# Attention scores of a graph network layer: destination rows from a reversed scan of on-chip rows instead of gathers, batches in descending order

## The chip, the core and the metric

The kernel runs on one core of a Trainium2 chip. The metric is device time in microseconds (us). A core has five engines, each with its own instruction queue: PE (TensorE, matmuls and transposes), DVE (VectorE), ACT (ScalarE), POOL (GpSimd, here the issuer of the indirect DMAs that gather or scatter rows) and SP (SyncE, here the issuer of plain DMAs). They meet through semaphores alone. SBUF is the on-chip memory, PSUM the eight banks that PE writes.

## What is computed

Four graph layers over 50,000 nodes of 128 numbers and 25,000 edges that are sorted by destination; after each layer the result is added to x and normalised row by row. The change concerns the third layer:

```python
h = jnp.einsum('nd,rde->rne', x, W)              # W: 8 relations, 128 x 128
h_src, h_dst = h[edge_type, src], h[edge_type, dst]
attn = jnp.sum(h_src * h_dst, axis=-1)
attn = jax.nn.leaky_relu(attn, negative_slope=0.2)
# softmax of attn over the edges of each type -> a
out = jax.ops.segment_sum(h_src * a[:, None], dst, num_segments=N)
```

## The kernel before

The edges are padded to 49 batches (`NB`) of 512 (`BE`), each of four tiles (`BT`) of 128. The stages run one after the other, with a barrier between them: setup (columns of flags and row numbers), prefill, CONV1, CONV2, MEAN, attention scores, softmax, ATTEND, SUM. In MEAN, ATTEND and SUM (`edge_stage`) a batch's gathered source rows are turned on PE into columns, DVE writes a copy for each relation in which only that relation's edges are not zero (`masked`, L1302), PE multiplies it by that relation's weights and adds up (L1225), DVE sums over equal destinations with a forward scan (L1323), and PE turns the sums back into rows (L1215).

MEAN leaves two things for the attention stage. The table X2 in HBM holds one finished row for each node; for a node with edges it is the row written at its last edge. The SBUF buffer `m.xd` holds, for each of the 25,088 edge places, the row that MEAN computed at that place; only at the last edge of a destination is that the destination's finished row.

The attention stage (`attention_stage`) computes x_dst (W_r W_rᵀ) x_src for each edge. After `ww` = W_r W_rᵀ is made, each of the 49 batches passes through:

- ACT writes the row numbers as integers, of the sources and of the destinations (L1518, L1519, `gi`).
- POOL gathers 4 tiles of source rows and 4 tiles of destination rows, one indirect DMA each (L1496, `rows`). SP stores the source rows to `source_rows` for ATTEND (L1479).
- PE transposes all 8 tiles (L1575) into the banks `T[0]` and `T[1]`; ACT copies both to SBUF (L1529, L1530, `col`). There is one such pair of banks, so the next batch's transposes wait for these copies.
- DVE makes 8 masks from the destination columns (L1592), PE multiplies each by `ww` (L1553, 16 instructions a batch, since each f32 matmul is two), DVE multiplies the sum by the source columns (L1603, `prod`), and PE adds that over the 128 features against a column of ones (L1564); ACT keeps the four columns of scores (L1523).

The order on each engine is the order of the code in its `body(b, q)`, which serves several batches at once: PE's body b does the scores of batch b-2, relations 0 to 3 of batch b, the transposes of b+1, relations 4 to 7 of b. `rows`, `gi` and `typ` have two slots, so the gathers for batch s wait until batch s-2 has been turned and its source rows stored. `hold` is a wait on SP or POOL.

## Time and profile before

| what | value |
|---|---|
| median of 3 runs | 3763.21 us (3763.13 to 3765.24) |
| profiled execution, its own time | 3760.51 us |
| its span, first to last instruction | 3758.6 us |
| PE busy | 2909.0 us, 77% |
| DVE busy | 2965.8 us, 79% |
| POOL busy | 1858.1 us, 49% |
| attention stage, first gather to last score | 1986.8 to 2521.3 us |

The profiled execution is one run of its own; its time stands 2.7 us under the median of the other three. Busy shares are means over stages that have different limits, so they don't say what bounds the attention stage.

### The profile page before, as it was taken

What the parts mean: (1) busy time and instruction counts of PE and PEld (TensorE: products, weight loads), DVE (VectorE), ACT (ScalarE), POOL (GpSimd) and SP (SyncE); (2) the same over time, 40 slices, a digit from 0 to 9 for tenths busy, and PEclk for the clock granted to TensorE, in tenths of its full rate; (3) what the DMA queues carried; (4) which work ended last, traced back from release to release, by engine and by line L of the source; (5) the groups of instructions that cost most, each with busy time, mean ns of one, the idle gap of its engine ahead of it and who ended that gap; (6) DMA issues with size and microseconds to landing.
All of it is one profiled execution on the core that took longest, in us unless ns stands there. A gap on an engine that the chain in (4) does not pass through costs nothing. (4 is left out here: it accounts for less than half of the span.)

```text
span 3758.6 us, 57586 instructions
## 1 busy us (share of the span) xinstructions
PE 2909.0 (77%) x10747; PEld 1631.2 (43%) x10747; DVE 2965.8 (79%) x8628; ACT 1678.5 (45%) x4665; POOL 1858.1 (49%) x1779
## 2 busy tenths in 40 slices
PE   2665664666655566799986888877999899999997
PEld 1433443555545555344433444443343344444443
DVE  7886555999969999699983555557999878888886
ACT  2775775888857677455541111113444411111111
POOL 2775776444434443355536777750000046666664
PEclk9998887889878887799998999988999999999998
DMA  2664444555545655233322222222222211111111
GB/s 64 198 194 147 150 150 134 190 198 199 198 139 193 197 185 186 94 92 92 92 82 80 87 88 86 83 61 66 92 92 85 86 49 45 46 50 49 50 53 34
DMA packets 267148, 418.71 MB, mean 111 GB/s; under 512 B 54780, under 2 KB 116537, under 8 KB 267082
## 3 DMA queue, kind: packets, MB, share of 16 engines
q1 hardware_dynamic: 210634, 318.80, 25.9%
q0 software_dynamic: 56448, 99.21, 9.5%
q8 instruction: 20, 0.33, 0.0%
q14 instruction: 46, 0.38, 0.0%
HBM read 215.60 MB, written 206.07 MB: 112 GB/s over the span
## 5 line engine op out<-in xcount | busy, mean ns | idle before, releaser
L1225 PE MATMUL bank<-sum_masked,sum_w 128*128 128x512 f32 x1568 | 691.1, 594 | 1.4 <-DVE sum_masked L1302 1.4
L1112 POOL DMA_INDIRECT sum_rows<-t_x,sum_gi x196 | 228.1, 1164 | 691.8 <-ACT sum_gi L1136 646.7
L1302 DVE SCALAR_TENSOR_TENSOR sum_masked<-sum_typ,sum_col 128x512 f32<-128x512 bf16 x784 | 487.9, 683 | 18.9 <-ACT sum_col L1155 16.9
L1496 POOL DMA_INDIRECT at_rows<-t_x,at_gi x392 | 391.5, 999 | 172.9 <-issue 124.5
L1592 DVE SCALAR_TENSOR_TENSOR at_masked<-at_typ,at_col 128x512 f32<-128x512 bf16 x392 | 247.0, 691 | 260.1 <-ACT at_col L1530 234.6
L1225 PEld LDWEIGHTS bank<-sum_masked,sum_w 128*128 128x128 f32 x1568 | 291.2, 191 | 332.2 <-issue 271.3
L1225 PE MATMUL bank<-mean_masked,mean_w 128*128 128x512 f32 x784 | 377.5, 612 | 18.8 <-DVE mean_masked L1302 18.8
L1225 PE MATMUL bank<-att_masked,att_w 128*128 128x512 f32 x784 | 380.4, 613 | 9.7 <-DVE att_masked L1302 7.7
L1553 PE MATMUL bank<-at_masked,at_ww 128*128 128x512 f32 x784 | 377.7, 627 | 1.9 <-DVE at_masked L1592 1.9
L1112 POOL DMA_INDIRECT mean_rows<-t_x,mean_gi x196 | 224.0, 1143 | 232.8 <-ACT mean_gi L1136 185.4
L1112 POOL DMA_INDIRECT c_rows<-t_g,c_gi x196 | 187.1, 955 | 274.9 <-ACT c_gi L1136 138.3
L920 ACT ACTIVATE c_dense_x<-c_dense_z,c_dense_shift,c_dense_scale 128x128 f32<-128x128 f32 x784 | 311.5, 480 | 16.9 <-DVE c_dense_shift L965 16.6
L1112 POOL DMA_INDIRECT c_rows<-x_dram,c_gi x196 | 189.6, 967 | 225.4 <-ACT c_gi L1136 177.5
L1155 ACT ACTIVATE sum_col<-bank 128x512 f32<-128x512 f32 x49 | 29.3, 597 | 571.4 <-PE bank L1265 571.4
L1120 POOL DMA_INDIRECT out_dram<-sum_new,sum_si x196 | 239.2, 1220 | 84.1 <-issue 57.9
L1302 DVE SCALAR_TENSOR_TENSOR mean_masked<-mean_typ,mean_col 128x512 f32<-128x512 bf16 x392 | 250.1, 680 | 17.7 <-ACT mean_col L1155 17.6
L1302 DVE SCALAR_TENSOR_TENSOR att_masked<-att_typ,att_col 128x512 f32<-128x512 bf16 x392 | 250.4, 681 | 12.7 <-ACT att_col L1155 12.4
L628 POOL DMA_INDIRECT pf_ds<-t_info,pf_gi x196 | 194.5, 992 | 84.6 <-issue 61.4
L626 POOL DMA_INDIRECT pf_xs<-x_dram,pf_gi x196 | 200.6, 1023 | 63.5 <-issue 57.4
L1553 PEld LDWEIGHTS bank<-at_masked,at_ww 128*128 128x128 f32 x784 | 150.6, 202 | 157.3 <-issue 126.7
L1225 PEld LDWEIGHTS bank<-mean_masked,mean_w 128*128 128x128 f32 x784 | 130.2, 190 | 197.1 <-DVE mean_masked L1302 153.0
L1225 PEld LDWEIGHTS bank<-att_masked,att_w 128*128 128x128 f32 x784 | 130.1, 190 | 191.1 <-DVE att_masked L1302 147.0
(289 smaller groups left out, 5696.2 us busy)
## 6 DMA issues: line engine op xcount, KB each, us to landing
t_x<-c_dense_x SPq DMA_DIRECT2D x196, 256.0 KB, 3.7
pf_xc<-x_dram SPq DMA_DIRECT2D x98, 256.0 KB, 3.0
t_g<-pf_g SPq DMA_DIRECT2D x98, 256.0 KB, 3.1
t_x<-pf_x SPq DMA_DIRECT2D x98, 256.0 KB
c_dense_x<-t_x SPq DMA_DIRECT2D x98, 256.0 KB, 3.8
out_dram<-c_dense_x SPq DMA_DIRECT2D x98, 256.0 KB, 4.0
c_same<-p_same SPq DMA_DIRECT2D x98, 128.0 KB, 3.5
t_g<-c_new SPq DMA_DIRECT2D x49, 256.0 KB
```

Of the source, the lines that this page charges most:

```text
L626: pool.indirect_dma_start(xs[:, q, j, :], None, io["x"], index).then_inc(gathered[q], 16)
L628: pool.indirect_dma_start(ds[:, q, j, :], None, m.info_table, index).then_inc(gathered[q], 16)
L920: last = act.activation(rows[:, q, j, :], self.z[:, q, j, :], ACT.Identity, bias=self.shift[:, q, i, j:j + 1], scale=self.scale[:, q, i, j ...
L1112: pool.indirect_dma_start(rows[:, q, j, :], None, source, bass.IndirectOffsetOnAxis(ap=gi[:, q, j:j + 1], axis=0))\
L1120: pool.indirect_dma_start(out, bass.IndirectOffsetOnAxis(ap=si[:, qs, j:j + 1], axis=0), new[:, qs, j, :], None, bounds_check=NP - 1, oob_ ...
L1155: act.activation(col[:, o, :], T[o][:, :], ACT.Copy).then_inc(col_ready, 1)
L1225: pe.matmul(H[q][:, :], w[:, r, :], masked[:, r % MASKS, :], start=(r == 0), stop=(r == n_rel - 1))\
L1302: v.scalar_tensor_tensor(out=masked[:, r % MASKS, :], in0=typ[:, q, :], scalar=float(r), in1=col[:, q, :], op0=ALU.is_equal, op1=ALU.mult) ...
L1496: pool.indirect_dma_start(rows[:, q, side, j, :], None, m.tables["X2"], bass.IndirectOffsetOnAxis(ap=gi[:, q, side, j:j + 1], axis=0))\
L1553: pe.matmul(U[q][:, :], ww[:, r, :], masked[:, r % MASKS, :], start=(r == 0), stop=(r == R8 - 1))\
L1592: v.scalar_tensor_tensor(out=masked[:, r % MASKS, :], in0=typ[:, q, :], scalar=float(r), in1=col[:, q, 1, :], op0=ALU.is_equal, op1=ALU.mu ...
```

## The change

The attention stage gathers only the source rows. The destination rows come from `m.xd`: ACT copies the batch's four tiles multiplied by a column that is 1 at the last edge of a destination and 0 elsewhere (`ends_col`, L1506 after the change), so all other rows become zero; PE transposes them into banks of their own (`turn_dst`, L1551), and DVE spreads each finished row back over all edges of its destination with a scan that runs from the last column to the first (`last_rows_back`, L1604), steered by a plane that is 1 where the next edge has the same destination (`next_plane`, loaded by SP). The scan carries its value from batch to batch, so the batches run from 48 down to 0. The roles of the two sides swap: the masks are made of the source columns, and `prod` multiplies by the destination columns. Setup loses the computation of the last edge's row number and its column, and gains the plane and the column of flags.

```diff
-        SRC_F, CL_F, LAST_F, DINV_F, T8_F, DST_F, WEIGHT_F, END_F = range(8)
+        SRC_F, CL_F, LAST_F, DINV_F, T8_F, DST_F, WEIGHT_F = range(7)
...
-            for f, plane in enumerate((m.same_plane, m.type_plane[R8], m.type_plane[R16])):
+            for f, plane in enumerate((m.same_plane, m.type_plane[R8], m.type_plane[R16], m.next_plane)):
                 sp.dma_start(plane.rearrange("(q n) -> q n", n=256), typ[:, f, :]).then_inc(stored, 16)
-            hold(sp, stored, 48)
+            hold(sp, stored, 64)
...
+            v.tensor_copy(typ[:, 3, :], nxt[:, :])
...
-            v.wait_ge(numbered, 1)
-            link(v.scalar_tensor_tensor(out=end[:, :], in0=cnt[:, 1, R8, :], scalar=-1.0, in1=number[:, :],
-                                        op0=ALU.add, op1=ALU.add))
-            link(slot_rows(v, end_rows, end[:, :]))
-            link(v.tensor_tensor(own[:, :], end_rows[:, 0, :], end_rows[:, 1, :], ALU.add))
-            v.scalar_tensor_tensor(out=field[:, END_F, :], in0=own[:, :], scalar=float(NP), in1=end_rows[:, 2, :],
-                                   op0=ALU.add, op1=ALU.add)
...
-            v.wait_ge(colC, 8)
+            v.wait_ge(colC, 7)
+            v.tensor_scalar(m.ends_col[:, :], m.last_col[:, :], float(FAR), None, ALU.is_lt)
...
+        T, TD, U, SC, WB = m.psum[0:2], m.psum[2:4], m.psum[4:6], m.psum[6:8], m.psum[2:4]
         LAST = NB - 1
+        batch = lambda s: s * -1 + LAST
...
                 if runs(s, 0, LAST):
                     if runs(s, 2):
                         hold(sp, mask_ready, (s - 1) * R8)
-                    plane = m.type_plane[R8][bass.ds(s * BE, BE)]
-                    sp.dma_start(typ[:, q, :], plane.rearrange("(a n) -> a n", a=1).to_broadcast([P, BE]))\
-                        .then_inc(typ_loaded[q], 16)
+                        hold(sp, dst_ready, s - 1)
+                    sp.dma_start(typ[:, q, :], spread(m.type_plane[R8], s)).then_inc(typ_loaded[q], 16)
+                    sp.dma_start(nxt[:, q, :], spread(m.next_plane, s)).then_inc(nxt_loaded[q], 16)
                 s = b + 1
                 if runs(s, 0, LAST):
-                    hold(sp, gathered[1 - q], of_slot(s, 1 - q, 32 * BT))
-                    sp.dma_start(m.source_rows[:, bass.ds(s * BE, BE)],
-                                 rows[:, 1 - q, 0].rearrange("p b d -> p (b d)")).then_inc(stored[1 - q], 16)
+                    hold(sp, gathered[1 - q], of_slot(s, 1 - q, 16 * BT))
+                    sp.dma_start(m.source_rows[:, bass.ds(batch(s) * BE, BE)],
+                                 rows[:, 1 - q].rearrange("p b d -> p (b d)")).then_inc(stored[1 - q], 16)
...
-                        hold(pool, turned, s - 1)
+                        hold(pool, src_turned, s - 1)
                         hold(pool, stored[q], of_slot(s - 2, q, 16))
-                    for side in range(2):
-                        for j in range(BT):
-                            pool.indirect_dma_start(rows[:, q, side, j, :], None, m.tables["X2"],
-                                                    bass.IndirectOffsetOnAxis(ap=gi[:, q, side, j:j + 1], axis=0))\
-                                .then_inc(gathered[q], 16)
+                    for j in range(BT):
+                        pool.indirect_dma_start(rows[:, q, j, :], None, m.tables["X2"],
+                                                bass.IndirectOffsetOnAxis(ap=gi[:, q, j:j + 1], axis=0))\
+                            .then_inc(gathered[q], 16)
...
                     if runs(s, 2):
-                        act.wait_ge(gathered[q], of_slot(s - 2, q, 32 * BT))
-                    act.activation(gi[:, q, 0, :], at(m.row_col, s), ACT.Copy)
-                    act.activation(gi[:, q, 1, :], at(m.end_col, s), ACT.Copy).then_inc(idx_ready, 1)
+                        act.wait_ge(gathered[q], of_slot(s - 2, q, 16 * BT))
+                    act.activation(gi[:, q, :], at(m.row_col, batch(s)), ACT.Copy).then_inc(idx_ready, 1)
+                    if runs(s, 2):
+                        act.wait_ge(dst_turned, s - 1)
+                    for j in range(BT):
+                        last = act.activation(ends[:, q, j, :], m.xd[:, bass.ds(batch(s) * BE + j * D, D)], ACT.Copy,
+                                              scale=m.ends_col[:, bass.ds(batch(s) * BT + j, 1)])
+                    last.then_inc(ends_ready, 1)
...
-                    act.wait_ge(turned, s + 1)
+                    act.wait_ge(src_turned, s + 1)
                     if runs(s, 2):
-                        act.wait_ge(prod_ready, s - 1)
-                    act.activation(col[:, o, 0, :], T[0][:, :], ACT.Copy)
-                    act.activation(col[:, o, 1, :], T[1][:, :], ACT.Copy).then_inc(col_ready, 1)
+                        act.wait_ge(mask_ready, (s - 1) * R8)
+                    act.activation(col[:, o, :], T[o][:, :], ACT.Copy).then_inc(col_ready, 1)
...
+            def turn_dst(s, q):
+                if not runs(s, 0, LAST):
+                    return
+                pe.wait_ge(ends_ready, s + 1)
+                if runs(s, 2):
+                    pe.wait_ge(dst_ready, s - 1)
+                for j in range(BT):
+                    last = pe.transpose(TD[q][:, j * TE:(j + 1) * TE], ends[:, q, j, :], m.ident[:, :])
+                last.then_inc(dst_turned, 1)
+
...
-                    pe.wait_ge(gathered[o], of_slot(s, o, 32 * BT))
-                    if runs(s, 1):
-                        pe.wait_ge(col_ready, s)
-                    for side in range(2):
-                        for j in range(BT):
-                            last = pe.transpose(T[side][:, j * TE:(j + 1) * TE], rows[:, o, side, j, :], m.ident[:, :])
-                    last.then_inc(turned, 1)
+                    pe.wait_ge(gathered[o], of_slot(s, o, 16 * BT))
+                    if runs(s, 2):
+                        pe.wait_ge(col_ready, s - 1)
+                    for j in range(BT):
+                        last = pe.transpose(T[o][:, j * TE:(j + 1) * TE], rows[:, o, j, :], m.ident[:, :])
+                    last.then_inc(src_turned, 1)
+                turn_dst(s, o)
                 relate(b, q, range(R8 // 2, R8))
...
-                                           in1=col[:, q, 1, :], op0=ALU.is_equal, op1=ALU.mult).then_inc(mask_ready, 1)
+                                           in1=col[:, q, :], op0=ALU.is_equal, op1=ALU.mult).then_inc(mask_ready, 1)
+
+            def last_rows_back(s, q):
+
+                if not runs(s, 0, LAST):
+                    return
+                v.wait_ge(nxt_loaded[q], of_slot(s, q, 16))
+                v.wait_ge(dst_turned, s + 1)
+                if runs(s, 1):
+                    v.wait_ge(dst_ready, s)
+                if runs(s, 2):
+                    v.wait_ge(prod_ready, s - 1)
+                start = 0.0 if static(s) and s == 0 else dst[:, 1 - q, 0:1]
+                v.tensor_tensor_scan(dst[:, q, ::-1], nxt[:, q, ::-1], TD[q][:, ::-1], start, ALU.mult, ALU.add)\
+                    .then_inc(dst_ready, 1)
...
                 s = b - 1
                 if runs(s, 0, LAST):
                     v.wait_ge(mask_used, (s + 1) * R8)
+                    v.wait_ge(dst_ready, s + 1)
                     if runs(s, 2):
                         v.wait_ge(scored, s - 1)
-                    v.tensor_tensor(prod[:, o, :], col[:, o, 0, :], U[o][:, :], ALU.mult).then_inc(prod_ready, 1)
+                    v.tensor_tensor(prod[:, o, :], dst[:, o, :], U[o][:, :], ALU.mult).then_inc(prod_ready, 1)
+                last_rows_back(b, q)
                 relate(b, q, range(R8 // 2, R8))
```

On PE, two bodies that stand written out ahead of the loop. The names are those of the tiles: `at_masked` the masks, `at_prod` the products, `at_rows` the gathered rows, `at_ends` the flagged rows of `m.xd`. Before:

```order
L1553 MATMUL bank<-at_masked,at_ww 128x512 x4
L1564 MATMUL bank<-m_ones,at_prod 128x1 x4
L1553 MATMUL bank<-at_masked,at_ww 128x512 x4
L1575 MATMUL bank<-m_ident,at_rows 128x128 x8
L1553 MATMUL bank<-at_masked,at_ww 128x512 x4
L1564 MATMUL bank<-m_ones,at_prod 128x1 x4
L1553 MATMUL bank<-at_masked,at_ww 128x512 x4
L1575 MATMUL bank<-m_ident,at_rows 128x128 x8
L1553 MATMUL bank<-at_masked,at_ww 128x512 x4
```

and after:

```order
L1541 MATMUL bank<-at_masked,at_ww 128x512 x4
L1562 MATMUL bank<-m_ones,at_prod 128x1 x4
L1541 MATMUL bank<-at_masked,at_ww 128x512 x4
L1572 MATMUL bank<-m_ident,at_rows 128x128 x4
L1551 MATMUL bank<-m_ident,at_ends 128x128 x4
L1541 MATMUL bank<-at_masked,at_ww 128x512 x4
L1562 MATMUL bank<-m_ones,at_prod 128x1 x4
L1541 MATMUL bank<-at_masked,at_ww 128x512 x4
L1572 MATMUL bank<-m_ident,at_rows 128x128 x4
L1551 MATMUL bank<-m_ident,at_ends 128x128 x4
L1541 MATMUL bank<-at_masked,at_ww 128x512 x4
```

The eight transposes of gathered rows have become four of gathered rows and four of `at_ends`, behind a wait of their own; nothing else on PE has moved.

On SP, the issues of the batches written out ahead of the loop, before:

```order
L1479 DMA source_rows<-at_rows 128x512
L1474 DMA at_typ<-p_type 128x512
L1479 DMA source_rows<-at_rows 128x512
L1474 DMA at_typ<-p_type 128x512
L1479 DMA source_rows<-at_rows 128x512
L1474 DMA at_typ<-p_type 128x512
```

and after (`at_nxt` is the plane's slot):

```order
L1464 DMA source_rows<-at_rows 128x512
L1459 DMA at_typ<-p_type 128x512
L1460 DMA at_nxt<-p_next 128x512
L1464 DMA source_rows<-at_rows 128x512
L1459 DMA at_typ<-p_type 128x512
L1460 DMA at_nxt<-p_next 128x512
L1464 DMA source_rows<-at_rows 128x512
```

One more load stands in front of each store of the source rows.

On DVE, the first batches, written out ahead of the loop (x8 is masks 4 to 7 of one batch and 0 to 3 of the next), before:

```order
L1592 SCALAR_TENSOR_TENSOR at_masked<-at_typ,at_col 128x512 x12
L1603 TENSOR_TENSOR at_prod<-at_col,bank 128x512
L1592 SCALAR_TENSOR_TENSOR at_masked<-at_typ,at_col 128x512 x8
L1603 TENSOR_TENSOR at_prod<-at_col,bank 128x512
L1592 SCALAR_TENSOR_TENSOR at_masked<-at_typ,at_col 128x512 x8
```

and after:

```order
L1590 SCALAR_TENSOR_TENSOR at_masked<-at_typ,at_col 128x512 x4
L1604 SCALAR_TENSOR_TENSOR at_dst<-at_nxt,bank 128x512
L1590 SCALAR_TENSOR_TENSOR at_masked<-at_typ,at_col 128x512 x8
L1616 TENSOR_TENSOR at_prod<-at_dst,bank 128x512
L1604 SCALAR_TENSOR_TENSOR at_dst<-at_nxt,at_dst,bank 128x512
L1590 SCALAR_TENSOR_TENSOR at_masked<-at_typ,at_col 128x512 x8
L1616 TENSOR_TENSOR at_prod<-at_dst,bank 128x512
```

Behind each product the scan (the order prints a scan as SCALAR_TENSOR_TENSOR; `at_dst` is its output) has come in, ahead of masks 4 to 7.

## Rows read from the trace of the kernel before

**Rows 1.** Busy time in stretches: attention stage, then MEAN (PEclk is the granted clock)

```profile
1987.00:2520.00 533.00, 458.94 (x1560) 244.59 (x1560) 273.92 (x441) 70.02 (x239) 391.24 (x392) 0.93 0.28 84
1563.00:1965.00 402.00, 381.90 (x1114) 165.38 (x1114) 377.20 (x938) 204.40 (x552) 204.15 (x176) 1.00 0.30 89
```

**Rows 2.** Waits between 2010 and 2510 us: us in total, times, longest

```profile
PE bank L1575 <- DMA at_rows<-t_x,at_gi: 59.0, 33, 3.1
```

**Rows 3.** The gathers by tile: duration ns min/median/max, first and last start

```profile
L1496 POOL DMA_INDIRECT at_rows<-t_x,at_gi x392: 938/944/1459, 1986.8 to 2503.8; - x196
```

**Rows 4.** Timeline of a batch that waited: start us, us, engine, line

```profile
2347.45 1.97 PE L1575 MATMUL bank<-m_ident,at_rows 128*128 128x128 f32 x8 [2.92 <-DMA at_rows<-t_x,at_gi]
2349.21 5.70 PE L1553 MATMUL bank<-at_masked,at_ww 128*128 128x512 f32 x8
```

**Rows 5.** Stretch of the same batch, columns as in Rows 1

```profile
2348.00:2350.00 2.00, 2.00 (x8) 1.55 (x7) 0.00 (x0) 0.55 (x2) 1.39 (x3) 0.50 0.50 174
```

**Rows 6.** Timeline of PE in a batch that never waited

```profile
2355.55 3.68 PE L1553 MATMUL bank<-at_masked,at_ww 128*128 128x512 f32 x8
2359.07 1.04 PE L1575 MATMUL bank<-m_ident,at_rows 128*128 128x128 f32 x8
2359.94 3.60 PE L1553 MATMUL bank<-at_masked,at_ww 128*128 128x512 f32 x8
2363.38 0.95 PE L1564 MATMUL bank<-m_ones,at_prod 128*128 128x1 f32 x8
2364.19 3.68 PE L1553 MATMUL bank<-at_masked,at_ww 128*128 128x512 f32 x8
```

**Rows 7.** Timeline of ACT: score copy of batch 0 and of batch 46

```profile
2023.68 0.17 ACT L1523 ACTIVATE m_score_col<-bank 128x4 f32<-128x4 f32 x1 [2.95 <-PE bank L1564]
2512.35 0.17 ACT L1523 ACTIVATE m_score_col<-bank 128x4 f32<-128x4 f32 x1 [3.14 <-PE bank L1564]
```

**Rows 8.** DVE beside the PE of Rows 6, and ACT's column copy

```profile
2364.04 0.68 DVE L1603 TENSOR_TENSOR at_prod<-at_col,bank 128x512 f32<-128x512 f32 x1
2364.64 2.49 DVE L1592 SCALAR_TENSOR_TENSOR at_masked<-at_typ,at_col 128x512 f32<-128x512 bf16 x4
2368.78 0.60 ACT L1529 ACTIVATE at_col<-bank 128x512 f32<-128x512 f32 x1 [4.14 <-PE bank L1575]
```

**Rows 9.** Scans: setup forward, setup backward, MEAN forward from PSUM

```profile
22.09 0.67 DVE L392 TENSOR_TENSOR_SCAN su_cnt<-su_flag,su_relid 98x256 f32<-98x256 f32 x1
22.67 0.67 DVE L393 TENSOR_TENSOR_SCAN su_cnt<-su_flag,su_relid 98x256 f32<-98x256 f32 x1
L1323 DVE TENSOR_TENSOR_SCAN mean_run<-mean_same,mean_run,bank x48: 1278/1279/1281, 1557.6 to 1960.8; 128x512 f32<-128x512 bf16 x48
```

**Rows 10.** Timeline: ACT's scaled row copies in ATTEND, four tiles

```profile
2704.37 1.28 ACT L1148 ACTIVATE att_scaled<-att_rows,m_alpha_col 128x128 f32<-128x128 f32 x4 [3.10 <-DMA att_rows<-source_rows]
```

**Rows 11.** Timeline of the SUM stage: one group of four transposes, then relations

```profile
3410.55 0.60 PE L1215 MATMUL bank<-m_ident,sum_run 128*128 128x128 f32 x4
3410.98 7.03 PE L1225 MATMUL bank<-sum_masked,sum_w 128*128 128x512 f32 x16
```

**Rows 12.** DMA issues, 1990 to 2510 us: KB each, median us to landing

```profile
source_rows<-at_rows SPq DMA_DIRECT2D x49, 256.0 KB, 2.6
```

**Rows 13.** Timeline of the stage's start

```profile
1990.51 0.94 POOL L1496 DMA_INDIRECT at_rows<-t_x,at_gi  x1 [0.30 <-issue]
1995.50 0.94 POOL L1496 DMA_INDIRECT at_rows<-t_x,at_gi  x1 [0.30 <-issue]
1998.11 1.94 PE L1575 MATMUL bank<-m_ident,at_rows 128*128 128x128 f32 x8 [12.92 <-DMA at_rows<-t_x,at_gi]
2001.95 5.33 PE L1553 MATMUL bank<-at_masked,at_ww 128*128 128x512 f32 x8 [1.90 <-DVE at_masked L1592]
```

**Rows 14.** Timeline of setup on DVE: destination row numbers, up to the next sum

```profile
41.90 0.42 DVE L415 SCALAR_TENSOR_TENSOR su_end<-su_cnt,su_number 98x256 int32<-98x256 f32 x1
43.89 2.55 DVE L421 TENSOR_TENSOR su_cnt<-su_cnt 98x2304 f32<-98x2304 f32 x1
```

More of the change, by code:

```diff
@@ L322, in setup_stage @@
         carry = sb("carry", [QR, 2, R8 + 1])
-        field = sb("field", [QR, 8, 256])
-        typ = sb("typ", [QR, 3, 256], BF16)
+        field = sb("field", [QR, 7, 256])
+        typ = sb("typ", [QR, 4, 256], BF16)
         own = sb("own", [QR, 256])
@@ L327, in setup_stage @@
         rooted = sem("rooted")
-        numbered = sem("numbered")
-        number = sb("number", [QR, 256])
-        end = sb("end", [QR, 256], I32)
-        end_rows = sb("end_rows", [QR, 3, 256], I32)
         ps = m.psum
@@ L466, in _ @@
             pe.wait_ge(lin, 2)
-            for f in range(8):
+            for f in range(7):
                 for b in range(2):
@@ L1444, in attention_stage @@
         MASKS = 8
-        gi = sb("gi", [P, 2, 2, BT], I32)
-        rows = sb("rows", [P, 2, 2, BT, D])
-        typ = sb("typ", [P, 2, BE], BF16)
-        col = sb("col", [P, 2, 2, BE])
+        gi = sb("gi", [P, 2, BT], I32)
+        rows = sb("rows", [P, 2, BT, D])
+        typ, nxt = sb("typ", [P, 2, BE], BF16), sb("nxt", [P, 2, BE], BF16)
+        col, dst = sb("col", [P, 2, BE]), sb("dst", [P, 2, BE])
+        ends = sb("ends", [P, 2, BT, D])
         masked = sb("masked", [P, MASKS, BE])
@@ L1466, in _, with spread @@
             sp.dma_start(w[:, :, :], io["W_att"].rearrange("r i o -> i r o")).then_inc(w_loaded, 16)
+            def spread(plane, s):
+                return plane[bass.ds(batch(s) * BE, BE)].rearrange("(a n) -> a n", a=1).to_broadcast([P, BE])
             def body(b, q):
@@ L1711, in build @@
         m.dstraw_col, m.hi_col, m.lo_col, m.ds_col, m.score_col = map(column, ("dstraw", "hi", "lo", "ds", "score"))
-        m.weight_col, m.alpha_col, m.row_col, m.end_col = map(column, ("weight", "alpha", "row", "end"))
+        m.weight_col, m.alpha_col, m.row_col, m.ends_col = map(column, ("weight", "alpha", "row", "ends"))
         m.node = sb("node", [P, RPP])
```

19 lines of the change are left out of this document (8 added, 11 removed).

## The prediction

> **What bounds the kernel now.** I read the page's slices first: the attention stage lies between MEAN and softmax, and in it no engine is busy throughout. The windows say how far off PE is: 459 of 533 us busy at a mean granted clock of 0.93, where MEAN, with the same eight relations a batch, has 382 of 402 us at 1.00 [rows 1]. So PE is idle or slowed for part of the stage, and the question is what it waits for. The chain of what ended last is of no help here, as it lies in SUM and says nothing of an earlier stage; the waits inside the stage are. PE waits 59.0 us for the gathers, in 33 waits, the longest 3.1 us [rows 2].
>
> Then the gathers themselves: 392 of them start between 1986.8 and 2503.8 us, one each 517.0 / 391 = 1.322 us, though one lasts 0.944 [rows 3]. Eight a batch make 8 x 1.322 = 10.58 us. The score copies give the stage's rhythm: from that of batch 0 at 2023.68 to that of batch 46 at 2512.35 are 46 intervals, 10.62 us each [rows 7]. The two agree within 0.4%: **POOL's issue of the gathers is the bound**, with no room in it.
>
> PE pays twice for it. A batch that waited 2.92 us for its gathers turned its rows in 1.97 us and ran 8 matmul instructions in 5.70 [rows 4], with the granted clock at 0.50, that is 1.2 GHz [rows 5]; a batch without the wait took 1.04 and 3.60 for the same [rows 6]. Such a batch then runs late, and the next ones catch up. What PE needs when it never waits is in Rows 6: from one batch's first relation at 2355.55 to the next's at 2364.19 are **8.64 us** (3.52 for four relations, 0.87 for eight transposes, 3.44 for four relations, 0.81 for the scores). That is the floor of PE at 2.4 GHz.
>
> **What the change does to each engine, per batch.** POOL: four gathers of eight go, so 4 x 1.322 = 5.3 us of issue remain where 10.6 were. That is well under 8.64, so POOL no longer bounds, unless its waits do (below).
>
> PE: four transposes of gathered rows become four of flagged rows, the rest is the same; what is new is a second group with a wait of its own. SUM shows what a group of four costs when PE is the bound: from 3410.55 to 3410.98, 0.43 us [rows 11], so two groups are 0.86 against 0.87 for one of eight. I take 8.64. The other bound is that such a group costs the whole 0.60 us of its row instead of 0.43, if its wait keeps it from overlapping what follows: 0.17 us more, 8.81.
>
> DVE: adds the scan. Eight masks take 2 x 2.49, the product 0.68 [rows 8]. The scan isn't in the trace as it will run, backward from a PSUM bank. Two rows are near: MEAN's forward scan from PSUM of the same 512 elements takes 1.279 us, and setup's 256-element scans take 0.67 us forward and 0.67 backward [rows 9]. Direction costs nothing there, so I take 1.28; the upper end, twice the rate lost, is 2.56. Sum 4.98 + 0.68 + 1.28 = 6.9 us, below 8.64. Its place matters more than its sum: it stands between the product and masks 4 to 7. Counted from the start of PE's scores at 2363.38, the product starts at +0.66 and ends its turn at +1.26 [rows 6, 8]; the scan holds DVE to +2.54, mask 4 is there at about +3.2, masks 4 to 7 end at +5.0. PE asks for mask 4 at 0.81 + 3.52 + 0.87 = +5.2. There are 2.0 us to spare; a scan of 2.56 us leaves 0.7, so both ends give the same time. Masks 0 to 3 of the next batch need ACT's column copy, which comes at about +5.4 once four transposes, not eight, are done; they end by +8.0, before PE asks at +9.4.
>
> ACT: one column copy (0.60 [rows 8]) goes, four scaled row copies come, 1.28 us for the four in ATTEND [rows 10]. Together with the small ones some 2.3 us of work in 8.64. They are made a batch ahead, and wait only for transposes that PE has passed. They cost nothing, hidden by PE's matmuls; without that cover 1.3 us.
>
> SP: one more plane load per batch, ahead of the store of the source rows, and a wait for the scan. Behind that store the gathers two batches on wait, so this is the queue to check. Masks of batch b are done at +5.0 of body b, later than the scan, so the new wait is never the last. Allow 1 us for the two loads' issue (my choice, more than any issue here seems to need): the store goes out at +6.2 and lands 2.6 us later [rows 12], at +8.8. The gathers of batch b+3 then start, four at 1.322, the last at +12.8, and its rows come 2.6 us after its start (1995.50 to 1998.11 [rows 13]), at +15.4. PE wants them in body b+2, at 2 x 8.64 + 4.33 = +21.6. There are 6 us to spare.
>
> So no wait is left on PE, and with none the clock should stay where MEAN has it. **The stage's 46 intervals: 46 x (10.62 - 8.64) = 91.1 us less.**
>
> At this point the Trainium skill (TensorE: Matmul & The Clock Gate, section "HAM oscillation — how this bites in real kernels") tells of a matmul loop whose waits on DMAs each let the clock gate throttle PE, so that the next tile starts cold. The trace agrees: 2.92 us of wait, then 0.50. By that page the second payment of each wait goes too, which is within the 91.1.
>
> **The stage's start.** The first transposes wait for the last of batch 0's gathers. It was the eighth, started at 1995.50; now it is the fourth, as at 1990.51 [rows 13], 4.99 us earlier. Transposes at the low clock took 1.94 for eight, and two column copies stood before the first mask; with four (0.97) and one copy of 0.60 [rows 8], of which I count 0.5 as the two overlap a little, the first relation comes 1.47 us earlier again, at 2001.95 - 6.46 = 1995.49. From there to the score copy of batch 0 were 21.73 us, with waits for the next batches' gathers. Without them: 5.33 for the first eight instructions at the low clock [rows 13], 0.87 + 3.52 to the end of the batch, 8.64 - 0.81 for batch 1, and 0.95 for the scores ahead of the copy: 18.5. So 3.2 us less, 9.7 us for the start.
>
> **Setup.** The row numbers of the last edges go: 43.89 - 41.90 = 1.99 us [rows 14], and one copy of a column. Added are a copy to the plane and the column of flags. No row shows these three; at the 0.42 us of L415 each they come to 0.42 more added than removed, so 1.6 us less in sum, and 2.4 with the two new ones at nothing. I take 1.9, all on DVE's chain that ends setup.
>
> **Sum.** 91.1 + 9.7 + 1.9 = 102.7, from 3760.5, the profiled execution's own time: 3657.8. The median of the runs lies 2.7 us higher, which makes 3660.5; with some tenths for stray waits (a choice) I say 3661. All other stages have the same instructions.
>
> **Rivals.**
> 1. *PE still waits at times (SP's store or a group's wait late).* For it: before, each wait of 2 to 3 us cost as much again in clock, so the price per case is high. Against: 6 us to spare on the gathers and 2 on the masks. With the 8.81 bound at each batch it is 46 x 0.17 = 8 us: 3669. If every fourth batch lost 4 us (a wait and its low clock), 46: about 3707. Chance 0.10.
> 2. *The clock stays low without waits.* The skill's same page (section "A second HAM failure mode: psum-queue depth-cycling") has short idles between groups of matmuls, cycling through PSUM banks, make the clock oscillate. As a mechanism here: PE goes through four pairs of banks per batch, and breaks off before each group. Were the granted clock 0.93 as now, an interval would be 8.64 / 0.93 = 9.29, and 46 x 0.65 = 30 us are lost: 3691. Against it: MEAN cycles through its banks at 1.00 [rows 1]. Chance 0.05.
> 3. *The backward scan from PSUM is slow.* Up to some 3.3 us (1.28 + 2.0 to spare) it costs nothing. Beyond, DVE delays masks 4 to 7 by each us, and over a batch sum of 8.64 it is the bound. To end **slower than before**, the interval must exceed 10.62 + 11.5 / 46 + 0.16 = 11.0 us, so the scan 11.0 - 5.7 = 5.3 us, four times MEAN's. Setup's equal pair speaks against it; that pair read SBUF, not PSUM, so it doesn't exclude it. A scan of 4.5 us would give about 46 x 1.5 = 69 us over forecast, 3730. Chance 0.02 for slower, 0.01 for between.
> 4. *No change*: PE's wait is put on the gathers, but something else of 10.6 us is behind. Only POOL has a sum near it. Chance 0.02.
>
> **How the numbers follow.** Forecast 0.80, rivals 0.10, 0.05, 0.03 (0.01 and 0.02) and 0.02. The forecast's own range is 3654 (the start and setup at their best, no stray wait) to 3669 (8.81 each). To leave out no more than 2 in 10, the range goes up into rival 1 but not to rival 2's end: 3652 to 3686. A measurement of this kernel tells 0.2% or 7.5 us from no change. Faster: the forecast, rivals 1 and 2 and the 0.01 of rival 3, 0.96; same 0.02; slower 0.02.
>
> **What would show it.** Right: score copies 8.6 to 8.8 us apart, the granted clock 1.00 in the stage, no wait of PE on `at_rows`, POOL idle for about 3 us a batch, a scan near 1.28 us, DVE waiting for ACT's column copy as before but briefly, and the stage's last score near 2419 us. Wrong: a wait of PE on masks 4 or `at_ends` (the scan or ACT is late), on `at_rows` (SP's store), or long relations without a wait (the clock).

## The result, and the profile after

The changed kernel takes 3679.86 us (median of 4 runs, 3675.34 to 3687.97) against 3763.17 (4 runs, 3761.50 to 3765.24) before: ratio 0.9781, 95% interval 0.9762 to 0.9799. That is faster, inside the forecast's range (3652 to 3686) but 19 us above its 3661. The profiled execution took 3677.66, with a span of 3675.9, so it is 82.8 us shorter than that of before, where the sum had said 102.7. The question is where 20 us are.

Windows of the trace after: attention stage, its steady part, MEAN. Columns as in [rows 1].

```profile
1985.00:2520.00 535.00, 487.52 (x1734) 262.14 (x1735) 408.18 (x635) 128.26 (x406) 196.37 (x195) 0.95 0.28 81
2010.00:2400.00 390.00, 390.00 (x1446) 215.16 (x1444) 306.22 (x452) 91.95 (x310) 181.34 (x180) 1.00 0.31 92
1558.00:1960.00 402.00, 383.74 (x1122) 166.26 (x1120) 377.67 (x938) 204.68 (x552) 204.66 (x176) 1.00 0.31 89
```

The first row spans what the stage took before, and runs on into ATTEND. The second is the one to read: PE is busy for 390.00 of 390.00 us at a granted clock of 1.00, the upper of its two levels, 2.4 GHz. POOL is busy for 181 of 390 us (46%), where it was for 391 of 533 (73%) in [rows 1].

Four of the waits after, 2010 to 2400 us (total, times, longest):

```profile
ACT at_col L1518 <- PE bank L1572: 169.7, 45, 3.8
POOL at_rows L1480 <- DMA source_rows<-at_rows: 164.5, 45, 4.5
DVE at_masked L1590 <- ACT at_col L1518: 57.3, 45, 1.4
DVE at_prod L1616 <- PE bank L1541: 25.9, 45, 0.7
```

The view has no wait of PE itself in this stretch, neither on `at_rows`, as in [rows 2], nor on anything else. All four waiters here are engines with time over. POOL now waits for the store of the source rows, 164.5 / 45 = 3.7 us a batch, for which nobody waits in turn.

The tiles, after: gathers, the backward scan, the score copies (duration in ns min/median/max, first and last start).

```profile
L1480 POOL DMA_INDIRECT at_rows<-t_x,at_gi x196: 938/944/1468, 1983.5 to 2396.9; - x196
L1604 DVE TENSOR_TENSOR_SCAN at_dst<-at_nxt,at_dst,bank x48: 1272/1274/1275, 2004.4 to 2409.3; 128x512 f32<-128x512 bf16 x48
L1512 ACT ACTIVATE m_score_col<-bank x49: 173/173/174, 2012.3 to 2418.3; 128x4 f32 x42, 128x4 f32<-128x4 f32 x7
```

The scan backward from PSUM takes 1274 ns, MEAN's forward one 1279 [rows 9]. One batch in the timeline (start, duration, engine, line), which answers to [rows 6] and [rows 8]:

```profile
2201.28 0.95 PE L1562 MATMUL bank<-m_ones,at_prod 128*128 128x1 f32 x8
2201.57 0.69 DVE L1616 TENSOR_TENSOR at_prod<-at_dst,bank 128x512 f32<-128x512 f32 x1 [0.57 <-PE bank L1541]
2202.09 3.68 PE L1541 MATMUL bank<-at_masked,at_ww 128*128 128x512 f32 x8
2202.18 1.27 DVE L1604 TENSOR_TENSOR_SCAN at_dst<-at_nxt,at_dst,bank 128x512 f32<-128x512 bf16 x1
2202.49 0.94 POOL L1480 DMA_INDIRECT at_rows<-t_x,at_gi  x1 [3.26 <-DMA source_rows<-at_rows]
2203.37 2.51 DVE L1590 SCALAR_TENSOR_TENSOR at_masked<-at_typ,at_col 128x512 f32<-128x512 bf16 x4
2205.61 0.60 PE L1572 MATMUL bank<-m_ident,at_rows 128*128 128x128 f32 x4
2206.05 0.60 PE L1551 MATMUL bank<-m_ident,at_ends 128*128 128x128 f32 x4
2206.49 3.60 PE L1541 MATMUL bank<-at_masked,at_ww 128*128 128x512 f32 x8
```

The order on DVE is product, scan, masks 4 to 7, as reckoned. The two groups of transposes stand 0.44 us apart (0.43 was taken). The score copies follow each other in 8.63 or 8.64 us, and the last is at 2418.33, where the prediction had "near 2419"; before it was at 2521.16. **So the whole gain was there at the end of the attention stage: 102.8 us.** Twenty microseconds of it are lost behind it, in code that the change doesn't touch.

`att_sd` is computed once a batch in ATTEND. Its row shows how long the stage takes; the second row is ACT's idle time until the source rows have landed, the third is PE's idle time until ACT's scaled copies of them are there (us, times). First before, then after:

```profile
L1175 ACT ACTIVATE att_sd<-att_mv,m_eps x49: 281/288/297, 2584.7 to 2996.3; 128x4 f32<-128x4 f32 x49
  DMA att_rows<-source_rows: 157.3, 48
  PE bank L1265: 19.0, 16
```

```profile
L1161 ACT ACTIVATE att_sd<-att_mv,m_eps x49: 282/288/298, 2482.1 to 2912.8; 128x4 f32<-128x4 f32 x49
  DMA att_rows<-source_rows: 177.4, 48
  PE bank L1251: 36.2, 32
```

411.6 us have become 430.7, 8.97 a batch where it was 8.58, at a granted clock of 1.00 in both. PE waits 17.2 us more for the scaled copies. One load of the source rows and the scaled copies that wait for it, after; before, the copies started 3.57 us after the load's issue (2700.80 to 2704.37, [rows 10]):

```profile
2604.36 0.33 SPq L1068 DMA_DIRECT2D att_rows<-source_rows  x1
2608.95 1.28 ACT L1134 ACTIVATE att_scaled<-att_rows,m_alpha_col 128x128 f32<-128x128 f32 x4 [4.12 <-DMA att_rows<-source_rows]
2610.28 0.66 PE L1251 MATMUL bank<-m_ident,att_scaled 128*128 128x128 f32 x4 [1.07 <-ACT att_scaled L1134]
```

Now 4.59 us, and PE waits 1.07 us for the copies. Most such cases lie in every other batch of the stage's first three quarters; `att_sd` then comes 9.2 to 10.5 us after its forerunner, otherwise mostly 8.6 to 9.1. One more thing differs, and far ahead of the attention stage: in MEAN the plane of "same row as before" lands later. Landings of `mean_same`, issue to landing in us min/median/max, before and then after:

```profile
DMA to landing us min/median/max: 3.0/3.1/4.0
```

```profile
DMA to landing us min/median/max: 3.0/4.0/6.2
```

MEAN hides it: from first to last `mean_sd` it takes 404.5 us in both kernels. So what slows the loads is there before the attention stage has run, which speaks against anything that this stage leaves behind, and for the new HBM tensor `p_next`. The change declares it between `p_same` and `p_type8`.

### The profile page after: what moved, and what is told of

Its sections match the earlier page's. It is cut to its first block and busy times, and to the rows that moved or that the text cites. A ratio compares the mean times of both kernels' runs of the same rounds, so it can differ in the third digit from the quotient of the medians.

```text
span 3675.9 us, 58023 instructions
## 1 busy us (share of the span) xinstructions
PE 2871.5 (78%) x10745; PEld 1619.7 (44%) x10745; DVE 3024.5 (82%) x8672; ACT 1709.1 (46%) x4763; POOL 1659.8 (45%) x1582
## 3 DMA queue, kind: packets, MB, share of 16 engines
q1 hardware_dynamic: 217802, 325.28, 27.5%
q0 software_dynamic: 50176, 86.35, 8.5%
## 5 line engine op out<-in xcount | busy, mean ns | idle before, releaser
L1541 PE MATMUL bank<-at_masked,at_ww 128*128 128x512 f32 x784 | 359.0, 602 | 0.6 <-DVE at_masked L1590 0.6
L1480 POOL DMA_INDIRECT at_rows<-t_x,at_gi x196 | 197.6, 1008 | 262.7 <-DMA source_rows<-at_rows 169.1
L1288 DVE SCALAR_TENSOR_TENSOR att_masked<-att_typ,att_col 128x512 f32<-128x512 bf16 x392 | 249.9, 680 | 12.8 <-ACT att_col L1141 12.6
L614 POOL DMA_INDIRECT pf_ds<-t_info,pf_gi x196 | 194.4, 992 | 84.5 <-issue 60.9
L1541 PEld LDWEIGHTS bank<-at_masked,at_ww 128*128 128x128 f32 x784 | 142.9, 192 | 144.0 <-issue 119.3
```

The costliest lines, as they stand in the source:

```text
L614: pool.indirect_dma_start(ds[:, q, j, :], None, m.info_table, index).then_inc(gathered[q], 16)
L1288: v.scalar_tensor_tensor(out=masked[:, r % MASKS, :], in0=typ[:, q, :], scalar=float(r), in1=col[:, q, :], op0=ALU.is_equal, op1=ALU.mult) ...
L1480: pool.indirect_dma_start(rows[:, q, j, :], None, m.tables["X2"], bass.IndirectOffsetOnAxis(ap=gi[:, q, j:j + 1], axis=0))\
L1541: pe.matmul(U[q][:, :], ww[:, r, :], masked[:, r % MASKS, :], start=(r == 0), stop=(r == R8 - 1))\
```

## The experiments

The HBM tensors are declared in the order `p_same`, (`p_next`), `p_type8`, `p_type16`, `source_rows`. A plane has 25,088 numbers of 2 bytes, 50,176 bytes. "Distance" below is that from the start of `p_same` to that of `p_type8`, worked out on the footing that tensors lie in the order of their declaration; no trace shows an address.

### Is it the place of the new tensor?

**e1_plane_last**: the changed kernel with the one line moved.

```diff
-    m.next_plane = dram("p_next", (EP,), BF16)
     m.type_plane = {R8: dram("p_type8", (EP,), BF16), R16: dram("p_type16", (EP,), BF16)}
     m.source_rows = dram("source_rows", (P, KT * D))
     m.records = dram("records", (EP, 4), I32)
     m.sorted_dst = dram("sorted_dst", (EP,), I32)
+    m.next_plane = dram("p_next", (EP,), BF16)
```

> The changed kernel with one difference: the HBM tensor of the new plane is declared last instead of between the planes of before, so that every older HBM tensor stands where it stood before the change; work, order and DMAs are the same. Theory A (the loads of ATTEND land later because the tensors moved in HBM): ATTEND's intervals go back from 9.2 to about 8.75 us on average, and the kernel from 3680 to about 3661. Theory B (the count or order of DMAs issued earlier decides how a load lands): no difference, 3675 to 3688. Theory C (something that the attention stage leaves behind, such as the order in which source_rows was written): no difference either.

Measured: 3662.17 us (5 runs, 3660.68 to 3664.11), ratio 0.9736 (0.9723 to 0.9748) to the kernel before on the same chip. The 17.7 us are back, and the forecast's 3661 with them.

```profile
L1161 ACT ACTIVATE att_sd<-att_mv,m_eps x49: 281/288/298, 2481.8 to 2896.6; 128x4 f32<-128x4 f32 x49
```

ATTEND takes 414.8 us here, 15.9 less than in the changed kernel; that is all but 1.8 of the difference.

**e2_before_plane_between** and **e3_before_plane_last**: the kernel *before*, with the same tensor and one store into it in setup, which nothing reads. They differ in where it is declared, as in the changed kernel or as in e1.

```diff
-            hold(sp, stored, 48)
+            sp.dma_start(m.next_plane.rearrange("(q n) -> q n", n=256), typ[:, 0, :]).then_inc(stored, 16)
+            hold(sp, stored, 64)
```

> The kernel before with the new plane's HBM tensor put where the change puts it, and one store into it in setup (nothing reads it); gathers and order as before. Theory A (place in HBM): ATTEND slows by about 19 us with nothing else changed, the kernel goes from 3763 to about 3782. Theory B (one DMA more): the same slowing can come from the additional store, so the next kernel is needed beside it. Theory C (the attention stage leaves it behind): 3763, no difference.

> The kernel before with the same additional tensor and store, but the tensor declared last, so that nothing older moves in HBM. Theory A: 3763, as before. Theory B (one DMA more): as slow as the kernel with the tensor in between, about 3782. Theory C: 3763.

Measured: e2 3777.18 us (5 runs, 3776.18 to 3780.16), ratio 1.0041 (1.0028 to 1.0054); e3 3760.55 (12 runs, 3755.36 to 3765.49), ratio 0.9999 (0.9990 to 1.0008). The kernel before, with its gathers and its old attention stage, becomes 16 us slower from a tensor that it doesn't read. Rows of e2:

```profile
L1176 ACT ACTIVATE att_sd<-att_mv,m_eps x49: 281/288/297, 2582.6 to 3014.7; 128x4 f32<-128x4 f32 x49
ACT att_scaled L1149 <- DMA att_rows<-source_rows: 149.8, 43, 4.7
DMA to landing us min/median/max: 3.0/4.0/5.3
DMA to landing us min/median/max: 3.3/3.6/6.0
```

ATTEND takes 432.1 us; the third row is `mean_same`, the fourth `att_rows`, which before had 3.1/3.4/4.8. With e3 the theories "one more store does it" and "the attention stage leaves something behind" are out.

### Which part of the place?

**e5_plane_behind_types** declares `p_next` behind the type planes, so that only `source_rows` and the two small tensors behind it stay moved; **e6_plane_padded** leaves it between but makes it larger; **e12_plane_ahead**, run later, declares it ahead of `p_same`, so that the type planes and `source_rows` lie as in the changed kernel and `p_same` is beside them again.

```diff
     m.same_plane = dram("p_same", (EP,), BF16)
-    m.next_plane = dram("p_next", (EP,), BF16)
+    m.next_plane = dram("p_next", (65536,), BF16)[0:EP]       # e6
```

```diff
+    m.next_plane = dram("p_next", (EP,), BF16)                # e12
     m.same_plane = dram("p_same", (EP,), BF16)
-    m.next_plane = dram("p_next", (EP,), BF16)
```

> The changed kernel with the new plane's HBM tensor declared behind the two type planes, so that the type planes stand where they stood before and source_rows (and the two small tensors behind it) are moved by the plane's 50,176 bytes. Theory A1 (the place of source_rows itself): slow as the changed kernel, about 3680. Theory A2 (the place of the type planes, whose loads run beside): 3662, as with the plane declared last.

> The changed kernel with the new plane's HBM tensor where the change has it, but 131,072 bytes long instead of 50,176, so that what stands behind it moves by a power of two. Theory A3 (what counts is the address below some power of two up to 131,072 bytes): about 3662. Theory A4 (any displacement does it, or the place counts in larger units): slower than that, by up to 18 us, 3680.

> The changed kernel with the new plane's HBM tensor declared ahead of the plane of equal destinations, so that the type planes and source_rows stand exactly where the changed kernel has them, but the plane of equal destinations is again next to the type plane (50,176 bytes between their starts, not 100,352). Theory D (what counts is the distance between the two planes that are loaded side by side): 3662. Theory P (what counts is the place of the type planes itself): 3680.

All declarations together; ATTEND is first to last `att_sd`, of the profiled execution:

```
kernel        distance   mean_same median  ATTEND   time (us)  ratio (95%)
before          50,176   3.1               411.6    3763.17    1
changed        100,352   4.0               430.7    3679.86    0.9781 (0.9762-0.9799)
e1 last         50,176   3.2               414.8    3662.17    0.9736 (0.9723-0.9748)
e5 behind types 50,176   3.1               413.3    3663.05    0.9738 (0.9725-0.9751)
e6 padded      181,248   3.1               414.4    3664.94    0.9743 (0.9730-0.9757)
e12 ahead       50,176   3.1               412.7    3661.78    0.9730 (0.9716-0.9743)
e2 before+     100,352   4.0               432.1    3777.18    1.0041 (1.0028-1.0054)
e3 before+      50,176   3.1               413.6    3760.55    0.9999 (0.9990-1.0008)
```

e5 shows that where `source_rows` lies doesn't matter; e12 takes out the absolute place of the type planes alone. What the two slow kernels share, and none of the six others has, is `p_type8` 100,352 bytes behind `p_same`. The other six runs agree: e4, with this distance, has a `mean_same` median of 4.0, and e7 to e11, with 50,176, have 3.1. e6 shows that it isn't being apart as such.

**The distance alone isn't the rule, though.** Other loads of the same traces, for which nobody waits, show it. In the attention stage `at_nxt` (`p_next`) is issued right behind `at_typ` (`p_type8`). Its landings in the changed kernel (50,176 bytes apart), in e5 (`p_next` 100,352 behind) and in e6 (131,072 ahead):

```profile
DMA to landing us min/median/max: 3.1/3.3/3.7
DMA to landing us min/median/max: 3.9/4.3/5.2
DMA to landing us min/median/max: 4.0/4.3/4.9
```

So 131,072 can be as slow as 100,352, and 100,352 isn't slow throughout: in e12 `p_next` is that far ahead of `p_type8`, and, read load by load, the first nine batches (48 to 40, at the end of the planes) land in 4.3 to 5.0 us, the other forty in 3.1 to 3.8.

In the changed kernel's MEAN the distance is the same for all batches, yet `mean_same` lands in 3.9 us or more up to batch 38 and in 3.0 to 3.6 from batch 40 on (the trace has the landing of every second load).

In SUM the load beside `p_same` is that of `p_type16`, 100,352 bytes behind it in the kernel before, in e1 and in e12, and 231,424 in e6. `sum_same` in these four, in this order:

```profile
DMA to landing us min/median/max: 2.9/3.2/5.0
DMA to landing us min/median/max: 2.9/3.2/4.8
DMA to landing us min/median/max: 2.9/3.0/4.9
DMA to landing us min/median/max: 2.9/4.1/4.7
```

The medians hide a pattern: in the kernel before and in e1 every second load, up to batch 38, lands in 3.9 to 5.1 us and the ones between in 2.9 to 3.4; in e6 the trace has only the first kind. In e12, at the same distance but with both planes 50,176 bytes further on, all but the first land in 2.9 to 3.5.

So late landings of this sort were there before the change, in a stage that doesn't wait for them; and something besides the distance counts, such as the place of the pair. One regularity is left: e6 has the type planes 131,072 bytes behind where e1 has them, and lands as e1 does in MEAN (in time) and in SUM (late up to batch 38). That is what theory A3 said; e6 is its only test. What in the memory makes it so stays open.

The Trainium skill (DMA: Bandwidth & Descriptors, section "Latency and other measured facts") has the latency of HBM rise with its load, from 0.2 to 2 us. This pair isn't explained by load: the DMA engines' share in ATTEND is 0.29 in the changed kernel (2490 to 2890 us) and 0.28 before (2590 to 2990).

### Can the late landing be hidden?

**e4_rows_first** and **e11_plane_last_rows_first**: SP issues ATTEND's load of the source rows ahead of the load of the type plane, not behind it (with the wait that belongs to each); e4 on the changed kernel, e11 on e1.

```diff
+                    if kind == ATTEND:
+                        if runs(s, 2):
+                            hold(sp, scaled_ready, s - 1)
+                        sp.dma_start(flat(rows[:, q]), m.source_rows[:, bass.ds(s * BE, BE)]).then_inc(rows_loaded[q], 16)
                     if n_rel:
                         if runs(s, 2):
                             hold(sp, mask_ready, (s - 1) * n_rel)
                         sp.dma_start(typ[:, q, :], spread(m.type_plane[n_rel], s)).then_inc(typ_loaded[q], 16)
-                    if kind == ATTEND:
-                        ...
```

> The changed kernel with SP's load of ATTEND's rows issued ahead of the load of the type plane, which waits for all masks of the batch before; the rows' load then goes out several us earlier and no longer ends ACT's wait. If the late rows are what makes ATTEND slower (all theories of the cause share this), ATTEND's intervals fall to about 8.5 us as in MEAN, some 34 us less than in the changed kernel: about 3646. If instead ATTEND is slow for another reason (the scan's plane or the type plane landing late, or DVE itself), it stays near 3680.

> Both remedies at once: the new plane's tensor declared last (3662 us alone) and ATTEND's rows loaded ahead of the type plane (3655 alone). If both act on the same late landing, and ATTEND is then bound by DVE as MEAN is (8.46 to 8.7 us an interval), 3645 to 3654, the fastest version; if the order alone already hides all of it, the same 3655 as with the order alone.

Measured: e4 3654.74 us (5 runs, 3651.82 to 3657.21), ratio 0.9715 (0.9703 to 0.9728); e11 3655.22 (5 runs, 3654.33 to 3658.19), ratio 0.9711 (0.9698 to 0.9724). Rows of e4, the second for `mean_same`, the third for `att_rows`:

```profile
L1161 ACT ACTIVATE att_sd<-att_mv,m_eps x49: 281/297/298, 2481.5 to 2888.2; 128x4 f32<-128x4 f32 x49
DMA to landing us min/median/max: 3.0/4.0/5.5
DMA to landing us min/median/max: 2.6/3.6/4.7
```

`mean_same` lands as late as in the changed kernel, and `att_rows` as late as in e2 (the trace of the changed kernel has no landing for it), yet ATTEND takes 406.7 us, 24.0 less than there and 8.1 less than e1. The load used to wait on SP for masks of the batch before; asked for earlier, it has the time to be late: PE waits for the scaled copies once, at the stage's start, and no more. With the order changed the place is worth nothing more: e4 and e11 are equal. Both are the fastest of all kernels here, 25 us below the change alone. Of e4's expectation the place in the order was right and the size too hopeful: the intervals alternate between 8.47 and 8.84 us for most of the stage.

### Was POOL's issue the bound?

**e7_four_more_gathers** and **e8_two_more_gathers**: e1 with four or two more gathers a batch, of rows that are gathered anyway, into a buffer that nothing reads. The arithmetic is that of e1.

```diff
+                    for j in range(4):      # e8: range(2)
+                        pool.indirect_dma_start(more[:, q, j, :], None, m.tables["X2"],
+                                                bass.IndirectOffsetOnAxis(ap=gi[:, q, j:j + 1], axis=0))\
+                            .then_inc(gathered[q], 16)
```

The waits on `gathered` in PE, ACT and SP, left out here, count the additional gathers as well, so PE waits for all eight (or six) as it did before.

> The changed kernel with the plane declared last (3662 us), and four more gathers a batch, of the same source rows into a buffer that nothing reads, so that POOL issues eight a batch as before while PE, DVE and ACT work as after. If the issue of gathers on POOL is what bounded the stage before: intervals of about 10.6 us, PE waiting for rows, the granted clock falling behind each wait, and the 91 us of the steady part plus some 5 us of the start back: 3753 to 3765. If it was the transposes, ACT's two copies or the one pair of banks: no more than the start's 5 us, 3667.

> The same with two more gathers a batch: six of 1.322 us are 7.9 us, under PE's 8.64. If POOL's sum decides, the intervals stay at 8.64 and only the start costs 2.5 us: 3663 to 3667. If the gathers are already short of time behind SP's store of the source rows (the start of the gathers waits for its landing), PE begins to wait: 3680 or more.

Measured: e7 3765.12 us (10 runs, 3760.64 to 3767.77), ratio 1.0010 (1.0000 to 1.0019): the whole gain is gone. e8 3662.25 (4 runs, 3658.15 to 3662.95), ratio 0.9734 (0.9719 to 0.9749): as e1. Rows of e7, from the waits (2010 to 2400 us), the window and the tile:

```profile
PE bank L1577 <- DMA at_more<-t_x,at_gi: 56.7, 30, 4.0
2010.00:2400.00 390.00, 332.63 (x1160) 176.34 (x1158) 249.29 (x366) 75.03 (x252) 297.60 (x292) 0.97 0.34 98
L1517 ACT ACTIVATE m_score_col<-bank x49: 173/174/175, 2020.2 to 2522.5; 128x4 f32 x42, 128x4 f32<-128x4 f32 x7
```

The same of e8:

```profile
2010.00:2400.00 390.00, 390.00 (x1445) 215.06 (x1444) 309.06 (x454) 93.19 (x315) 271.37 (x273) 1.00 0.36 106
L1517 ACT ACTIVATE m_score_col<-bank x49: 173/173/174, 2016.6 to 2422.6; 128x4 f32 x42, 128x4 f32<-128x4 f32 x7
```

Eight gathers a batch cost 8 x 1.322 = 10.6 us of issue, more than PE's 8.64, and PE waits again (56.7 us in 390, against 59.0 in 500 in [rows 2]) and its mean clock is 0.97. The score copies of batches 0 to 46 come 10.73 us apart on average, in e8 8.64. POOL is the one engine without time over in e7: of its 390 us it is busy for 298, idle for 91 between its own instructions with nothing to wait for, and waits for others 1.2. The load on the DMA engines isn't the cause, since their share is 0.34 in e7 and 0.36 in e8, which loses nothing. Six gathers cost 7.9 us, less than 8.64, and only the start moves: 29.8 us from first gather to first score copy, 27.5 in e1. So the threshold lies between six and eight, as the sums have it.

One thing of e7's expectation didn't hold: the clock doesn't fall behind each wait. Of the 39 stretches of 10 us between 2010 and 2400, seven have a mean clock of 0.83, the others 1.00; behind the wait of 1.79 us at 2227.91 eight matmul instructions ran in 3.60 us. In seven places, then, the wait-then-low-clock pattern of the section "HAM oscillation — how this bites in real kernels" (the Trainium skill, TensorE: Matmul & The Clock Gate) is seen here too: with waits 0.97 on average, without 1.00.

### How much can DVE take?

**e9_two_scans** and **e10_three_scans**: e1 with one or two more backward scans of the same rows ahead of the real one, into a buffer that nothing reads.

```diff
+                for i in range(2):          # e9: range(1)
+                    v.tensor_tensor_scan(again[:, q * 2 + i, ::-1], nxt[:, q, ::-1], TD[q][:, ::-1], 0.0, ALU.mult, ALU.add)
```

(Shown is e10; e9 makes one, into `again[:, 0]`.)

> The changed kernel with the plane declared last, and the backward scan made twice a batch (the first into a buffer that nothing reads), some 1.2 us more for DVE ahead of masks 4 to 7. By the prediction's sum there are 2.0 us to spare in front of mask 4 and 1.7 in DVE's total: no change, 3662. If DVE is closer to the bound than reckoned, the intervals grow by up to 1.2 us, 3718.

> The same with three scans, some 2.4 us more. DVE's sum becomes 4.98 + 0.68 + 3 x 1.2 = 9.3 us, over PE's 8.64: intervals of about 9.3 us and 3662 + 46 x 0.65 = 3692. If only the slack in front of mask 4 counts (0.4 us are missing there), 8.64 + 0.4 = 9.0 us and about 3680; if PE's clock falls in the new waits, well above 3700.

Measured: e9 3663.41 us (4 runs, 3659.89 to 3667.18), ratio 0.9737 (0.9722 to 0.9752), no change from e1. e10 3673.51 (4 runs, 3671.98 to 3677.32), ratio 0.9761 (0.9746 to 0.9776), 11.3 us above e1. DVE in e10:

```profile
2200.07 0.68 DVE L1619 TENSOR_TENSOR at_prod<-at_dst,bank 128x512 f32<-128x512 f32 x1
2200.67 2.32 DVE L1606 TENSOR_TENSOR_SCAN at_again<-at_nxt,bank 128x512 f32<-128x512 bf16 x2
2202.91 1.25 DVE L1607 TENSOR_TENSOR_SCAN at_dst<-at_nxt,at_dst,bank 128x512 f32<-128x512 bf16 x1
2204.08 4.96 DVE L1591 SCALAR_TENSOR_TENSOR at_masked<-at_typ,at_col 128x512 f32<-128x512 bf16 x8
2208.97 0.68 DVE L1619 TENSOR_TENSOR at_prod<-at_dst,bank 128x512 f32<-128x512 f32 x1
2010.00:2400.00 390.00, 388.90 (x1399) 209.39 (x1399) 389.27 (x526) 89.54 (x303) 174.39 (x175) 1.00 0.31 89
```

From product to product are 8.90 us without a gap: DVE is the bound, by 0.25 us over PE's 8.64. 46 x 0.25 = 11.5 us; between the medians it is 11.3, and in the trace the 46 intervals take 12.4 us more than in e1. The price was expected higher because the durations of the rows were summed. The starts say what an instruction takes of its engine when the next is ready: 1.12 us for a scan of 1.20 (2200.67 to 2202.91 for two), 1.17 for one of 1.25, 0.61 for a mask (4.89 for eight). The place of the scans added little: they put mask 4 back by 2.24 us, more than the 2.0 that the prediction had to spare there, but no wait on a mask is longer than 0.3 us, and DVE, busy for 389.27 of 390 us, is held by its sum.

## Why the prediction was right, and where it was off

**What bounds the kernel** was read rightly. POOL's issue set 10.62 us a batch. The 46 intervals went from 488.67 to 397.25 us, 91.4 less, where 91.1 was reckoned. e7 restores the sum on POOL with every other part of the change in place, and restores the time; e8 shows that POOL decides only above PE's 8.64.

**PE at 8.64 us a batch** held to 0.01 us for nearly all batches, with 0.43 for each group of transposes and the upper bound of 8.81 not needed. Rival 1 (PE still waits at times) and rival 2 (the clock stays low without waits) are out by the window: 390.00 of 390.00 us busy at 1.00, though PE goes through four pairs of banks a batch. Rival 1's "each wait of 2 to 3 us cost as much again in clock" was too strong: in the kernel before, eight matmul instructions behind a wait of 2.80 us at 2061.63 ran in 3.60 us, as without a wait.

**DVE, rival 3**: the scan from PSUM backward costs 1.274 us, as forward. The prediction's "Up to some 3.3 us (1.28 + 2.0 to spare) it costs nothing" looked at the place alone; its own sum allowed 8.64 - 4.98 - 0.68 = 3.0. The sum decides: e9, whose scans hold DVE for 2.3 us, loses nothing, and e10, with 3.4, loses 0.25 us a batch.

**SP**: the gathers wait for the store, and nobody for them in the steady part. There was less to spare than the 6 us of the sum. The store lands 3.4 us after its issue, not 2.6 (view of DMAs, 2010 to 2400 us), and in the steady part the last gather of a batch starts 6.0 to 7.9 us ahead of its transposes, nearly always 7.2 or more, where the sum had 21.6 - 12.8 = 8.8.

```profile
source_rows<-at_rows SPq DMA_DIRECT2D x45, 256.0 KB, 3.4
```

**Setup and the start**: the last score came 102.8 us earlier, where the terms made 102.7. To the tenth this is luck. Setup gave 2.0 (prefill begins at 60.9 instead of 62.9), as reckoned; the stages between scatter by more than that: in the seven kernels that have the changed attention stage without additions (after, e1, e4, e5, e6, e11, e12) the first gather starts at 1982.2 to 1988.2 us and the last score lies between 2417.1 and 2422.7. From first gather to first score copy it went from 36.9 us to 28.8, 8.1 less, where 9.7 was reckoned.

**The step that failed in size** is the last sentence of the sum: "All other stages have the same instructions." They have, and yet ATTEND took 430.7 us for 411.6. A term of zero should have been +19 in the profiled execution, and +16 to +18 by the runs that change only the tensor's place (e1, e2 against e3). The prediction had read `p_next` as a load and a store, not as something that moves its neighbours in HBM. Shown is that the place does it (e1, e2, e3) and that the wait it lengthens is ACT's for `att_rows` (e4 hides it). For `p_same` and `p_type8` in MEAN and ATTEND the one slow layout of the four tried is that with 100,352 bytes between them, in all fourteen kernels; the loads of the other stages show that the distance alone isn't the rule, and why a place can matter isn't shown.

The forecast of 3661 is what the change takes with its tensor in each of the four other places that were tried: 3662.17, 3663.05, 3664.94, 3661.78. The range held the changed kernel's time because rival 1 had stretched it upward. That was luck: cover for the wrong reason.

## What to carry to other kernels

Compare an engine's sum of issue over a batch with the sum of the engine that works next to it, and take both from starts, not from durations: here both thresholds (six gathers free, eight not; two scans free, three not) lay where the sums put them. A gain moves to the end of its stage intact and can be lost behind it, so after a change look at the stages that it didn't touch as well; landing times of loads in an earlier stage can show that what is late isn't of the changed stage's making. Look at them load by load, since a median over loads that alternate hides half of them. And where a load that is waited for stands in a queue behind one that isn't, change the two: that hid the whole loss, and gave 7 us more than that (3662.17 to 3654.74).

## What the runs showed of the hardware that was not expected

How two planes of 50,176 bytes, whose parts of 1 KB are spread to 128 partitions, lie to each other in HBM changes how fast they land, as far as the order of declaration tells where they lie; no trace shows an address. In MEAN `p_same` lands in 4.0 us (median) when `p_type8` begins 100,352 bytes behind it, and in 3.1 to 3.2 us at 50,176 or 181,248 bytes. It costs 16 to 18 us of some 3,700 in a stage that waits for such loads, with the same instructions, the same granted clock and about the same DMA share. The distance isn't the whole of it: `at_nxt` lands in 4.3 us at 100,352 (e5) and at 131,072 bytes (e6), and `sum_same` at 100,352 bytes lands late in every second batch (3.9 to 5.1 us, up to batch 38) in the kernel before and in 2.9 to 3.5 us in e12. And in the changed kernel's MEAN the late landings end at batch 40 of 49, with the distance unchanged.
